# Thin products of the delta-rule loop in another place of TensorE's order, and 32 more identity products per pass

## What is computed

```python
x = x + _L0_attn_ref(_layernorm(x), ...)     # gated delta rule: the loop that is changed
x = x + _L0_xattn_ref(_layernorm(x), ctx, ctx, ...)
x = x + _L0_ffn_ref(_layernorm(x), ...)      # 16 experts of width 64, top 4: identity products
...                                          # nine more sublayers, untouched
```

```python
def step(S, xs):
    q_t, k_t, v_t, g_t, b_t = xs
    S = S * jnp.exp(g_t)[..., None, None]
    kv = jnp.einsum('bhk,bhkv->bhv', k_t, S)
    S = S + jnp.einsum('bhk,bhv->bhkv', k_t, (v_t - kv) * b_t[..., None])
    o_t = jnp.einsum('bhk,bhkv->bhv', q_t, S)
    return (S, o_t)
...
o = o * rsqrt(mean(o * o) + EPS) * norm_w * silu(z)
return o.reshape(b_, t_, V_DIM) @ W_out
```

## Time and profile before

| what | value |
|---|---|
| median of three runs | 6015.92 us |
| profiled execution | 6025.72 us, span 6023.7 us |
| mean granted TensorE clock | 0.895 |
| PE busy | 5071.1 us (84%) |
| DVE busy | 3135.5 us (52%) |
| ACT busy | 1969.8 us (33%) |
| POOL busy | 849.6 us (14%) |

### The profile page before, as it was taken

One profiled execution on the slowest core, in us unless ns is written; L12 is line 12 of the kernel. 1 busy time (PEld: TensorE's weight loads), 2 busy tenths in 40 slices (PEclk: granted clock), 3 DMA queues, 4 the chain that ended last, 5 costly groups with the idle time before them and its releaser, 6 DMA issues. The chain is left out here.

```text
span 6023.7 us, 97485 instructions
## 1 busy us (share of the span) xinstructions
PE 5071.1 (84%) x36372; PEld 3031.4 (50%) x36372; DVE 3135.5 (52%) x7570; ACT 1969.8 (33%) x5136; POOL 849.6 (14%) x1328
## 2 busy tenths in 40 slices
PE   6988989768798898977879889897787988989778
PEld 4863444444486344444448633444445853344444
DVE  5654535644666453554466645455436654545543
ACT  3431414332343242433234323242323432324232
POOL 1420000120141000021024100002102410000210
PEclk7888999889698899988969899998896989999889
DMA  1000000001000000000100000000000000000000
GB/s 69 3 16 37 1 12 1 18 1 47 20 3 16 37 1 12 1 18 1 47 20 3 16 37 1 12 1 18 17 32 19 3 16 37 1 12 1 18 19 31
DMA packets 10597, 100.89 MB, mean 17 GB/s; under 512 B 1100, under 2 KB 5504, under 8 KB 6144
## 3 DMA queue, kind: packets, MB, share of 16 engines
q1 hardware_dynamic: 10112, 94.44, 4.1%
HBM read 93.39 MB, written 1.05 MB: 16 GB/s over the span
## 5 line engine op out<-in xcount | busy, mean ns | idle before, releaser
L88 PE MATMUL psum<-ident_bf 128*128 128x512 bf16 x1576 | 428.9, 426 | 162.7 <-DVE l_xattn_prob L517 48.0
L677 DVE TENSOR_REDUCE l_attn_peak<-psum 128x1 f32<-128x128 f32 (+3 forms) x512 | 249.3, 491 | 408.8 <-PE psum L613 408.1
L611 PE MATMUL psum<-l_attn_k_head,l_attn_q 128*128 128x128 f32 (+3 forms) x1024 | 410.5, 488 | 18.1 <-POOL l_attn_k_head L601 18.1
L88 PEld LDWEIGHTS psum<-ident_bf 128*128 128x128 bf16 x1576 | 156.3, 106 | 425.9 <-issue 150.1
L634 PE MATMUL psum<-l_attn_turned,l_attn_v 128*32 128x512 f32 (+3 forms) x1024 | 368.6, 444 | 0.0
L661 ACT ACTIVATE l_attn_prob<-psum,l_attn_peak 128x128 f32<-128x128 f32 (+3 forms) x512 | 269.6, 527 | 186.9 <-PE psum L622 155.7
L2454 DVE TENSOR_TENSOR l_attn_xx<-l_attn_xx,psum 128x256 f32<-128x256 f32 x512 | 207.8, 419 | 232.9 <-PE psum L2183 220.1
L332 ACT ACTIVATE l_ffn_silu<-psum 128x512 f32<-128x512 f32 (+2 forms) x216 | 128.9, 597 | 558.2 <-PE psum L302 558.2
L375 DVE TENSOR_TENSOR l_ffn_hidden<-l_ffn_silu,psum 128x512 f32<-128x512 f32 (+2 forms) x184 | 126.2, 686 | 326.5 <-ACT l_ffn_silu L332 326.4
L654 ACT ACTIVATE l_attn_turned<-psum 128x512 f32<-128x512 f32 (+3 forms) x512 | 221.8, 433 | 219.5 <-PE psum L622 219.3
L2179 PE MATMUL psum<-l_attn_ax,l_attn_xx 64*64 64x64 f32 x5120 | 279.3, 231 | 12.3 <-ACT l_attn_ax L2286 12.3
(11 more groups left out here) (473 smaller groups left out, 10230.1 us busy)
## 6 DMA issues: line engine op xcount, KB each, us to landing
streamed_weights<-pack_l_ffn SPq DMA_DIRECT2D x4, 5412.0 KB, 15.4
streamed_weights<-pack_l_ffn SPq DMA_DIRECT2D x4, 3972.0 KB, 12.0
streamed_weights<-pack_l_attn SPq DMA_DIRECT2D x5, 2848.5 KB, 9.7
streamed_weights<-pack_l_xattn SPq DMA_DIRECT2D x4, 2496.0 KB, 9.5
streamed_weights<-pack_l_ffn SPq DMA_DIRECT2D x4, 2192.0 KB, 8.3
streamed_weights<-pack_l_xattn SPq DMA_DIRECT2D x4, 2048.0 KB, 7.5
streamed_weights<-pack_l_ffn SPq DMA_DIRECT2D x4, 1667.5 KB, 6.5
w_const<-pack_const SPq DMA_DIRECT2D x1, 1524.0 KB, 6.6
```

What stands on the lines that cost most here:

```text
L88: pe.matmul(self.bank(bank), self.ident_bf[:, :], self.ident_bf[:, :].unsqueeze(1).to_broadcast([P, NT, P]), start=True, stop=True)
L611: pe.matmul(m.psum[:, bank_of_step(u), 0:(i + 1) * P], q_of(h)[:, i * P:(i + 1) * P], k_head[:, h % 2, 0:(i + 1) * P], start=True, stop=False)
L677: dve.tensor_reduce(peak[:, u:u + 1], m.psum[:, bank_of_step(u), 0:(i + 1) * P], AX, ALU.max, negate=True).then_inc(peak_ready, 1)
```

## The change

In TensorE's stream of the loop, the SECOND pairs' `corrected` goes from behind `whole_level` 5 to before it; their `output` goes from between `half_level` 6 and `whole_level` 6 to behind `whole_level` 5, before `half_level` 6; the `turn` of the SECOND pairs of the next step goes from before `whole_level` 6 to behind it. The first experts' stage issues 26 identity products in place of 18. The `z` block issues 24 identity products, into bank 4, before its product n = 4.

```diff
--- before.py
+++ after.py
@@ -276,7 +276,7 @@
                 def spread(g):
                     if g == 0:
                         if weigh_output:
-                            m.warm(pe, 18, 4)
+                            m.warm(pe, 26, 4)
                         pe.wait_ge(gate_ready, 1)
                         for t in range(NT):
                             ins = pe.transpose(m.psum[0:E, 6, t * P:(t + 1) * P], gate[:, t, :], m.ident)
@@ -2208,9 +2208,8 @@
                         elif l == 4:
                             past(n, add, FIRST)
                             coming(n, prep, SECOND)
-                        elif l == 6:
-                            past(n, output, SECOND)
-                            coming(n, turn, SECOND)
+                        elif l == 5:
+                            past(n, corrected, SECOND)
                         if n < STEPS:
                             whole_level(n, l)
                         if l == 1:
@@ -2220,8 +2219,9 @@
                         elif l == 4:
                             past(n, ks, SECOND)
                         elif l == 5:
-                            past(n, corrected, SECOND)
+                            past(n, output, SECOND)
                         elif l == 6:
+                            coming(n, turn, SECOND)
                             past(n, add, SECOND)
 
             @block.scalar
@@ -2511,6 +2511,8 @@
             def _(pe):
                 for n in range(2 * NT):
                     t, half = divmod(n, 2)
+                    if n == 4:
+                        m.warm(pe, 24, 4)
                     if n >= 2:
                         pe.wait_ge(z_ready, n - 1)
                     pe.matmul(m.bank(n % 2), m.xnT[:, tok(t)], w["z"][:, 512 * half:512 * half + 512], start=True,
```

## The result

| | before | after |
|---|---|---|
| median | 6016.35 us (4 runs) | 5973.18 us (4 runs, 5967.85 to 5985.39) |
| profiled span | 6023.7 us | 5968.5 us |
| mean granted TensorE clock | 0.895 | 0.912 |

What follows compares the result with a forecast made beforehand. The loop was taken as set by TensorE's own stream, losing to idle waits and half clock, with VectorE's chain the less visible bound. Loop 29, z block 8 and experts 15 us sum to 52: 6015.9 to 5964 us, range 5930 to 6000.

Steps and rivals of the forecast that it cites:

- The loop: First-layer loop, three reordered moves: 7.2 us gained per pass, 29 us in four passes.
- The cost of the order: Loop, VectorE's chain starting later: 0.15 us lost per step in steps 3 to 6, 0.75 us in 1 and 2.
- `half_level` of the next step then ends at about 286.65: Loop, step 4 into the next: end of the next half level in the new order, against 286.5 before at full clock.
- A push of over 0.4 us: Loop, VectorE's chain: a delay beyond the forecast 0.4 us would show the prediction wrong.
- The gain of the clock: Loop, half-clock loss per step: 1.25 us in place of 2.3 (steps 3 to 6) or 3.1 (steps 1, 2).
- Filling the 0.61 us wait: Loop, before `whole_level` 5: some 0.6 us of `corrected`'s 1.04 us falls into idle time, 0.4 us pushes the level back.
- The z block: 24 identity products in the z block's 7.65 us wait: 2.0 us gained per pass, 8 us in all.
- The experts: Eight more identity products in the experts' stage shorten the wait to 2.4 us: 4.9 us in three passes, 15 us.
- The one that the identity products have no effect: Z block and experts: identity products don't hold the clock, only the loop gains, 5987 us; chance 0.12.
- The slower one: Loop, behind level 6: more waits bring a longer fall, 10.2 us at half clock, 6045 us; chance 0.05.
- The 62 ns of issue for thin matmuls: Loop's thin products: issue-bound and alike at either clock, so the clock term would be nothing (neutral rival); no separate chance given.

Runs made afterwards that it cites:

- the kernel before with the small products: Twelve 128-column identity products added ahead of the SECOND turn's first pair, nothing moved, against the kernel before: 5961.3 us, ratio 0.9908.

## Why the prediction was right, and where it wasn't

- **The loop: right in sum, by errors that offset each other.** Forecast 29 us; the two profiles have 1023.6 and 991.4 us in four passes, 32 us, and the order alone measured 27 us. That the sum fits is in part luck. Over the four passes the steps 3 to 6 gave 20 us (14 forecast), the steps 1 and 2 gave 3 us (9 forecast), step 0 gave 4 us (2) and step 7 gave 5 us (4).
- **The cost of the order was under-sized.** I had 0.15 us per step in steps 3 to 6, where a step of the changed kernel with the clock at full takes 30.7 us and one of the kernel before with the small products 30.2 us: 0.5 us. In steps 1 and 2 it was 0.75 us, and it is 29.0 against 27.8 us: 1.2 us. The end of the order of before was nearly right (286.5; by the 11.29 us above it is 286.6). The failing term is "`half_level` of the next step then ends at about 286.65": with the measured 11.79 us it is 287.1. The chain starts 0.52 us later and not 0.4, and the last products end 0.66 us behind the fourth `part` (276.43 + 1.54 = 277.97, against 278.63) where I had 0.3. A push of over 0.4 us was among my signs of being wrong, and it came.
- **The gain of the clock was under-sized too.** I had one fall left in nearly every step, and half of the passes have none in the steps 3 to 6. The clock in the loop's windows is 0.96, 0.95, 0.92 and 0.94, where 0.91 to 0.93 was forecast. The fall in step 0, 6.8 us before and 3.4 us in three of the four passes now, had no term.
- **"Filling the 0.61 us wait" was counted as a gain; it is the loss.** The prediction saw that `corrected` delays VectorE, and took it as a small price of a move that helps. That move alone costs 27 us, and with `turn` 50 us (5952 to 6002). The prediction looked at `output` as what fills the time behind `whole_level` 5; `corrected` had been filling it already.
- **`turn`.** The prediction gave it no share of its own. It carries the gain: 64 us alone, and without it the other two moves give nothing.
- **The z block.** Forecast 2.0 us per pass, the stretch gives 2.3 us. The mechanism is as told: full clock at the last products, and the projection follows VectorE's end by 2.1 us. (4.06 us for 18 products are 0.226 us each and not 0.216; the 24 take 5.34 us.) By itself the edit measures 17 us, so some 8 us came from elsewhere, in stages that weren't edited; added to `turn` it measures nothing.
- **The experts.** Forecast 15 us, measured nothing. The wait is 2.44 us, as forecast. That a shorter wait brings a shorter stage isn't borne out: at 2.44 us the stage takes 56 or 61 us. The term was read off a single execution whose stage took 61.5 us in three passes, 4 us over what is usual. In the two profiles the stage still gives 12.9 us; the stretch ahead of the loop, which wasn't edited, gives another 10 us, and the stages behind the experts give some 9 us back.
- **The rivals.** The one that the identity products have no effect is right on the experts and wrong on the z block and, by the twelve small products, on the loop. The slower one, a longer fall where waits are packed more tightly, is what `corrected` alone does in part (falls of 6.8 us in most steps, 10.2 us in two). By the page "TensorE: Matmul & The Clock Gate" of the Trainium skill (in "A second HAM failure mode") short idle pieces between groups of matmuls make the clock swing; the runs agree in that twelve small products beside a wait of 0.94 us are worth 55 us, and the same waits with and without a fall in the changed kernel show that the pieces alone don't settle it. The 62 ns of issue for thin matmuls where hardware decode is off, in "Wait — 56ns, not 53.3ns?" of the same page of the Trainium skill, don't bind here: 32 products in 1.15 us are 36 ns each at full clock, and the loop's time moved with the clock.

## What to carry to other kernels

Where PE is nearly always busy with thin products and the granted clock falls once per step, look for the short waits ahead of the fall, and put useful work of the same step into them (`turn`: 64 us), or a few identity products (55 us). Before moving work into a wait, look at what it covers where it stands now, and on which engine the chain behind it starts; take the moves one by one and in pairs, since of three one may carry the gain, another take most of it back, and the third matter only beside the second. A stage time at a changing clock is one draw: read it in several passes or kernels before it becomes a term of a sum.

## What the runs showed of the hardware

The same code takes different times from pass to pass, depending on where the clock falls. The first experts' stage with 18 products takes 57.3 or 61.5 us. The cross attention in the profile of the z block alone differs by 2.7 us from pass to pass. The stretch from a pass's first product to the loop's first half level takes 104 to 109 us over the traces here. A change that shifts everything behind it moves these too, by some 10 us in sum here, in either direction. And I had not expected how much so little work does: twelve products of 128 columns, 0.84 us in a step of 30 us. With them in the order of before, the granted clock stayed at 2.4 GHz in the steps 3 to 6, but for one fall of 3.4 us in the four passes; without them it had fallen to 1.2 GHz for 3.4 or 6.8 us in each of these steps, behind a wait of 0.94 us.
